# Layer 3's rounding of the next weight chunk: the up and gate columns move ahead of the tile's own rounding on ScalarE

## What is computed

```
def _gemma_mlp(x, gate_w, up_w, down_w):
    g = jnp.einsum('bsh,hi->bsi', x, gate_w)
    u = jnp.einsum('bsh,hi->bsi', x, up_w)
    return jnp.einsum('bsi,ih->bsh', jax.nn.gelu(g, approximate=True) * u, down_w)
...
# cond: the two chosen skill experts, weighted, and the shared one (inner size 1024)
out, _ = jax.lax.scan(step, jnp.zeros_like(x), (skill_gate, skill_up, skill_down, dense_w.T))
out = out + _gemma_mlp(x, shared_gate, shared_up, shared_down)
...
# ffn: attention over the 16 heads of one token, then 8 gated 256x256 experts
att = jnp.einsum('bthd,btgd->bthg', q, k) / np.sqrt(HD).astype(np.float32)
att = jax.nn.softmax(att, axis=-1)
out = jnp.einsum('bthg,btgd->bthd', att, v).reshape(b, t, D)
x = x + (out @ Wo + bo)
gate = jax.nn.softmax(h2 @ Wg + bg, axis=-1)
combined = jnp.einsum('btd,edf,bte->btf', h2, We, gate)
```

## Time and profile before

| | |
|---|---|
| median of 3 runs | 1533.56 us (1532.3 to 1539.36) |
| the profiled execution's own time | 1535.98 us |
| its span in the trace | 1534.1 us |
| busy share PE / DVE / POOL / ACT | 86% / 67% / 46% / 39% |
| tiles of layer 3, first gelu to last | 841.0 to 1387.9 us |

### The profile page before, as it was taken

One profiled execution on the slowest core, in us unless ns is written; L12 is line 12 of the kernel. 1 busy time (PEld: TensorE's weight loads), 2 busy tenths in 40 slices (PEclk: granted clock), 3 DMA queues, 4 the chain that ended last, 5 costly groups with the idle time before them and its releaser, 6 DMA issues.

```text
span 1534.1 us, 18711 instructions
## 1 busy us (share of the span) xinstructions
PE 1321.8 (86%) x6536; PEld 1118.3 (73%) x6536; DVE 1030.5 (67%) x1854; ACT 591.7 (39%) x984; POOL 701.5 (46%) x371
## 2 busy tenths in 40 slices
PE   5999989999994799727888999988898979896698
PEld 4898776898782799715776788876687767774587
DVE  8499665499753555526766433498648884789887
ACT  3302422301420588604445455534552445342241
POOL 4320113720015467573002453386656674467790
PEclk9898987898985899958999999999999999996798
DMA  5300001400006699841000332221121222121000
GB/s 197 133 29 14 28 28 55 139 26 3 1 14 226 206 280 310 266 156 55 1 0 21 107 106 89 76 82 63 62 90 55 76 82 85 41 69 47 9 1 28
DMA packets 51773, 128.74 MB, mean 84 GB/s; under 512 B 6353, under 2 KB 30433, under 8 KB 51553
## 3 DMA queue, kind: packets, MB, share of 16 engines
q1 hardware_dynamic: 43840, 109.86, 22.0%
q0 software_dynamic: 4608, 12.59, 2.5%
q10 hardware_dynamic: 3232, 5.11, 0.9%
HBM read 105.25 MB, written 22.28 MB: 83 GB/s over the span
## 4 chain that ended last, share of the span: by engine, by line
PE 56%; DVE 16%; issue 10%; POOL 9%; ACT 4%; DMA 2%; another core or an unknown queue 2%; ACTq 1%; SPq 0%; POOLq 0%; DVEq 0%
PE bank L405 17%; PE bank L408 16%; PE bank L409 16%; POOL VW L458 4%; DVE bank L2335 2%; DVE G L458 1%; PE bank L804 1%; POOL w_lo L593 1%; DVE acc L2359 1%; DVE F L2359 1%; DVE acc L2628 1%; PE bank L953 1%; PE bank L774 1%; ACT w_hi L1601 1%
## 5 line engine op out<-in xcount | busy, mean ns | idle before, releaser
L405 PE MATMUL bank<-x_hi,w_hi 128*128 128x512 f32 (+1 forms) x560 | 221.6, 396 | 38.5 <-POOL w_lo L636 16.3
L636 POOL TENSOR_TENSOR w_lo<-raw,w_hi 128x1024 fp32r<-128x1024 f32 x48 | 117.7, 2453 | 226.5 <-ACT w_hi L1601 211.7
L408 PE MATMUL bank<-x_lo,w_hi 128*128 128x512 f32 (+1 forms) x560 | 215.4, 385 | 0.0
L409 PE MATMUL bank<-x_hi,w_lo 128*128 128x512 f32 (+1 forms) x560 | 214.6, 383 | 0.0
L405 PEld LDWEIGHTS bank<-x_hi,w_hi 128*128 128x128 f32 x560 | 111.8, 200 | 65.6 <-POOL w_lo L636 20.1
L405 PE MATMUL bank<-hid_hi,w_hi 128*128 128x512 f32 x328 | 134.3, 409 | 27.3 <-DVE hid_lo L2290 12.8
L1707 ACT ACTIVATE hid_hi<-bank 128x512 fp32r<-128x512 f32 x96 | 57.4, 598 | 196.4 <-DVE bank L2335 196.4
L409 PE MATMUL bank<-hid_hi,w_lo 128*128 128x512 f32 x328 | 131.8, 402 | 0.0
L408 PE MATMUL bank<-hid_lo,w_hi 128*128 128x512 f32 x328 | 131.8, 402 | 0.0
L409 PEld LDWEIGHTS bank<-x_hi,w_lo 128*128 128x128 f32 x560 | 111.5, 199 | 19.9
L408 PEld LDWEIGHTS bank<-x_lo,w_hi 128*128 128x128 f32 x560 | 111.9, 200 | 18.5
(11 more groups left out here) (473 smaller groups left out, 3643.6 us busy)
## 6 DMA issues: line engine op xcount, KB each, us to landing
raw<-in_skill SPq DMA_DIRECT2D x32, 768.0 KB
raw<-in_shared SPq DMA_DIRECT2D x16, 768.0 KB
raw<-in_l1e SPq DMA_DIRECT2D x20, 513.0 KB
base<-xs SPq DMA_DIRECT2D x38, 256.0 KB, 4.5
ys<-F SPq DMA_DIRECT2D x38, 256.0 KB, 5.0
VW<-in_l1e SPq DMA_DIRECT2D x18, 513.0 KB, 5.2
raw<-in_l0c SPq DMA_DIRECT2D x12, 512.0 KB
raw<-in_qkv SPq DMA_DIRECT2D x8, 768.0 KB
```

The source lines that it names most:

```text
L405: i = nc.tensor.matmul(out, sh, mh, start=first, stop=False)
L408: nc.tensor.matmul(out, sh, ml, start=False, stop=False)
L409: return nc.tensor.matmul(out, sl, mh, start=False, stop=last)
L636: nc.gpsimd.tensor_tensor(lo[:, UP3], src[:, UP3], hi[:, UP3].bitcast(F32), ALU.subtract).then_inc(w_up_ready.sem, 1)
```

## The change

In batches 1 to 3 (`b > 0`) `dense_hi(n)` is split. Its first part, the two waits and the rounding of the up and gate columns, is now issued straight behind the even tile's gelu, ahead of the wait for `g3_gated` and of the rounding to `hid_hi`. The rounding of the down columns stays behind `hid_hi`. Batch 0 is as it was. PE, DVE, POOL and SP have the same instructions in the same order.

```
-            def dense_hi(n):
+            def dense_hi(n, parts=(UP3, DOWN3)):
                 act.wait_ge(*raw_in[n % 2](0, raw_turn(CHUNKS + n)))
                 if n < W3_SLOTS:
                     act.wait_ge(*f2_down(BATCH - 1, 2 * n + 2))
                 else:
                     act.wait_ge(*d3_step(0, 2 * (n + 1 - W3_SLOTS)))
-                for part in (UP3, DOWN3):
+                for part in parts:
                     nc.scalar.activation(w_hi[n % W3_SLOTS][:, part], raw[n % 2][:, part], ACT.Copy
                                          ).then_inc(d3_hi.sem, 1)
...
                         nc.scalar.activation(gelu3[g % 2], PB[g % 2][0][:], ACT.Gelu_apprx_tanh).then_inc(g3_gelu.sem, 1)
+                        if next_chunk and b > 0:
+                            dense_hi(n, (UP3,))
                         act.wait_ge(*g3_gated(0, g + 1))
...
                     if next_chunk and b > 0:
-                        dense_hi(n)
+                        dense_hi(n, (DOWN3,))
```

## The result

The changed kernel takes 1540.55 us where the kernel before, timed beside it, takes 1527.77 (medians): the ratio on record is 1.0069, 95% interval 1.0045 to 1.0094, so about 10.5 us more (7 to 14). The two medians by themselves are 12.8 us apart (1.0084), inside that interval. One execution of 3191.29 us, in the slow state, is left out of the comparison. The profiled execution took 1543.41 us, its span 1541.4 (before: 1535.98 and 1534.1).

The account below looks back on a forecast made before the run. It took DVE to bound batch 1's attention steps and PE, DVE close behind, the experts' tiles. Terms -1.0 + 9.8 + 0.5 + 1.7 = +11.0 us on 1533.56 gave 1544.6 us, range 1531 to 1552.

Parts of the forecast that it names:

- Tile 12: Batches 2 and 3: earlier `w_lo` makes DVE's gate operations and product wait for POOL; +9.8 us for both.
- the last rival: DVE loses to POOL at every end, PE's clock adding where its idle time grows; +15 us or more, chance 0.09.
- Attention steps: Earlier `w_lo` shortens pairs of tiles, partly offset at each half's first step; -1.0 us, ends -4.4 and +2.4.
- the walk: One attention pair stepped through with profiled durations: the old loop less 0.22 us; 0.5 us early by batch 2's tile 3.
- Tiles 14 to 18: Batches 2 and 3: DVE waits up to 1.9 us for `w_lo`, mostly won back; +0.5 us in all (0 to 2).
- Tiles 20 to 23 of batch 3: DVE's product waits for POOL's second product, and POOL's next for a sum; +1.7 us (0 to 3.2).
- The chain simply gets shorter: Rival: earlier `w_lo` shortens the chain, at most 7.7 us over some 14 pairs; about 1526 to 1531, chance 0.11.
- POOL gets nothing between: Rival: at tile 12 DVE waits once for `w_lo`, then keeps the ports; +4.4 us, 1538, chance 0.20.
- DVE loses at every end: Rival: POOL runs several instructions while DVE waits, also in the steps; +15 us or more, 1549 to 1555, chance 0.09.
- Hidden anyway: Rival: DVE bounds where PE waits for `w_lo`, so the next common wait cancels changes; 1532 to 1535, chance 0.12.
- POOL's idle time before line 636: Sign in the changed trace: POOL's wait for ACT ahead of `w_lo` should fall well below 211.7 us.

Follow-up runs that it names:

- e2: The kernel before with the new order at tile 12 of batches 2 and 3 alone; ratio 1.0063 to the kernel before.
- e1: The changed kernel with the old order put back at tile 12 of batches 2 and 3; ratio 0.9985 to the kernel before.
- e4: The changed kernel, but at tile 12 of batches 2 and 3 POOL waits for DVE's product before starting `w_lo`; ratio 1.0009 to the kernel before.
- e12: The kernel before with the new order at tile 10 of batches 2 and 3 alone; ratio 0.9994 to the kernel before.
- e3: The kernel before with the new order in batch 1 alone; ratio 0.9966 to the kernel before.
- e5: The changed kernel with DVE's gate operations moved from tile 12 to tile 11, behind `hidden_lo`; ratio 1.0030 to the kernel before.
- e9: Repeat timing of the kernel before with the new order in batch 1 alone; ratio 0.9987 to the kernel before, interval 0.9966 to 1.0008.
- e8: The changed kernel with the old order at tiles 10 and 12 of batches 2 and 3; ratio 1.0011 to the kernel before.

## Why the prediction was right, and where it was not

**Tile 12: right in mechanism and size.** Predicted 1.7, 1.4 and 3.3 us for the three operations, and a wait of PE of 9; measured 1.66, 1.22, 3.28 and 8.64. The wait grew by 4.58 (predicted 4.9), and PE loses another 0.87 us behind it: in the stretch from gelu to gelu its busy time is 9.41 us instead of 8.54, at a granted clock of 0.73 instead of 0.86. In both kernels the clock falls to 1.2 GHz some 8.4 us behind the gelu. The kernel before has resumed by then, after 7.95 us; the changed one resumes after 12.53 and works on at the low clock for over 5 us. That I had only named under the last rival. Together 10.9 us against 9.8; e2, with the clock back earlier in one batch, has 9.8. e1, e2 and e4 show it from three sides.

**Attention steps: the right sign, mis-sized.** Predicted -1.0 us with -4.4 as its end. Eight traces with the new order have -3.3 us by tile 3 of batch 2, the same to 0.04. A pair in the middle gains 0.3, near the walk's 0.22. What the walk left out is the end of a half. The kernel before, order of time of DVE, tiles 17 and 18 of batch 1:

```profile
1035.08 1.22 DVE L2359 TENSOR_REDUCE F<-VW 128x64 f32<-128x1024 f32 x1 [0.58 <-POOL VW L458]
1037.45 1.22 DVE L2359 TENSOR_REDUCE F<-VW 128x64 f32<-128x1024 f32 x1 [0.49 <-POOL VW L458]
1040.43 1.73 DVE L2377 TENSOR_TENSOR F<-F,lg 128x1024 f32<-128x1024 f32 x1
```

The changed kernel, DVE and POOL at the same place, tile 18:

```profile
1027.81 1.21 DVE L2361 TENSOR_REDUCE F<-VW 128x64 f32<-128x1024 f32 x1
1029.12 1.30 POOL L639 TENSOR_TENSOR w_lo<-raw,w_hi 128x512 fp32r<-128x512 f32 x1
1030.78 1.23 DVE L2379 TENSOR_TENSOR F<-F,lg 128x1024 f32<-128x1024 f32 x1
```

DVE waited twice for POOL's last products, and its subtraction ahead of the softmax 0.5 us more for `w_lo`. With POOL ahead all three waits are gone. At the second crossing (tiles 0 to 6 of batch 3) e1, whose clock did not fall from tile 4 to 6, as that of the kernel before did not, goes from -3.03 at tile 4 to -4.10. With that it would be -4.4 us together, the far end of what I gave. But e1 is the exception: of the seven traces with the new order at tiles 0 and 2 of batch 3 the other six have a granted clock of 0.78 to 0.88 there and lose 0.5 to 3.3 us, while of the seven with the old order only e12's fell. Four of the six lose 0.5 to 0.6 us, and with that the steps gave -2.7. Whether the new order brings the clock down there, or chance did, no run separates.

**Tiles 14 to 18: right.** Predicted +0.5 (0 to 2); the changed kernel loses 0.6 us from tile 13 to 18 of batch 2 and 0.5 in batch 3. Another 0.7 is lost up to tile 0 of batch 3, and 0.6 given back by tile 4: +1.3 in all.

**Tiles 20 to 23 of batch 3: right in its range, with a part that I had not seen.** Predicted +1.7 (0 to 3.2) for a wait in the tiles. The wait is there: DVE's product takes 2.85 us instead of 1.24, and from tile 20 to 23 the gelus lose 1.3 us. From tile 18 to 20 they had gained 1.0, so from 18 to 23 it is 0.3. More comes one tile later (order of time, end of the stream, changed kernel):

```profile
1387.07 2.85 DVE L458 TENSOR_TENSOR G<-F,VW 128x1024 f32<-128x1024 f32 x1
1391.57 1.21 DVE L2361 TENSOR_REDUCE acc<-VW 128x64 f32<-128x1024 f32 x1
1392.92 2.41 POOL L458 TENSOR_TENSOR VW<-F,VW 128x1024 f32<-128x1024 f32 x1 [4.08 <-DVE acc L2361]
1393.35 3.06 DVE L458 TENSOR_TENSOR G<-F,VW 128x1024 f32<-128x1024 f32 x1
```

POOL's product waits for DVE's sum and then starts just ahead of DVE's, which takes 3.06 us; before, the one in this tile took 1.61. From the last gelu, the product of the next step but one starts after 11.62 us instead of 9.89: 1.7 us, and e1 has the same row with 11.63. So 2.0 in all.

**What the sum leaves.** Terms as measured: -4.4 + 10.9 + 1.3 + 2.0 = +9.8 us with e1's second crossing, +11.5 with -2.7 for the steps, against 10.5 timed (7 to 14) and 11.0 predicted. That the sum came so close is in part luck: the steps gave more than I took, tile 12 and the end cost more, and the two errors cancel. The forecast of 1544.6 us was 4 us above the measured 1540.55, as I had added the 11.0 to the 1533.56 of three runs, and the kernel before was at 1527.77 when timed beside the changed one. The profiled pair differs by more within the stream, +14.26. By the clock that execution of the changed kernel lost 3.3 us at tiles 4 to 6 of batch 3 and 1.6 twice between tiles 10 and 12, and the execution before lost 1.4 at tiles 3 to 6 of batch 2, where the changed one lost nothing.

**The rivals.** "The chain simply gets shorter" is true of batch 1 (e3) and fails at tile 12. "POOL gets nothing between" fails there, as the three rows alternate, and DVE goes ahead of POOL's next only in the steps, where its next operation is issued in time. "DVE loses at every end" falls with e5, though the row of 5.88 us it was taken from stays unexplained (last section). "Hidden anyway" falls with e1 against the changed kernel. One of my own signs was weak: POOL's idle time before line 636 should have fallen "well below" 211.7 us and is 193.1, since most of it lies where POOL has no other work.

## What to carry to other kernels

An engine that idles while it waits is not always on the path; ask who uses the ports in its idle time. Here POOL's late start kept a dependent row of small DVE operations clear of it, and each of them, however small, then waited for the end of a POOL instruction. Put such a row where POOL idles (e5), or hold POOL until it is through (e4), before an input of POOL is made earlier; here each took away more than half of the loss, and neither made the kernel faster than before (1.0030, 1.0009). And try an order tile by tile: the same edit brings some 2 us in one stage (the traces of e3 and e9) and loses about five times as much in another (e2).

## What the runs showed of the hardware

DVE and POOL take turns by what is issued. A DVE product that is already waiting when POOL's instruction ends goes next (e5 at 1122.65, and the changed kernel's step at 1017.49); an operation that is issued 0.1 us after POOL's next has begun waits for that one too. One kind of row speaks against this as a rule: at the end of the kernel DVE's `scalar_tensor_tensor` of 128x256 takes 5.88 us, from 1491.04 to 1496.92, and POOL began two further instructions, at 1492.00 and 1494.31, while it waited. At the same place of the changed kernel it takes 5.94. Why it did not get its turn is not shown. A `tensor_scalar` of 128x8 elements from SBUF with SBUF scalars is held like a `tensor_tensor` (5.37 us for four), a reduction and a reciprocal from SBUF are not (0.18).

PE's clock differs between executions of the same instructions. e1 and e8 have the same instructions up to tile 10 of batch 2, and stand there at -4.66 and -1.06 us; up to tile 3 they agree to 0.03. From there the clock fell to 1.2 GHz in one execution and not, or for a shorter time, in the other. A loss of 1.6 us between two stages in a single pair of profiles was such a fall here. A run with the edit at that place alone and a repeat without it showed that it comes with either order; only a count over all traces (8 of 12 against 2 of 16) says that the order may still bear on how often.
